# First two units of a mixture-of-experts layer routed inside the stage before it

## The reference, cut to what matters

```python
x = x + attn_a(layernorm(x))     # softmax attention + causal linear attention, one projection
x = x + ffn(layernorm(x))        # the feed-forward the change is about
x = x + attn_b(layernorm(x))     # state-space scan
x = x + ffn(layernorm(x))

def ffn(x):
    shared = (silu(x @ sw1) * (x @ sw2)) @ sw3
    probs = softmax(x @ rw + rb)                  # 8 experts
    w, idx = top_k(probs, 2); w = w / sum(w)
    # every expert: (silu(x @ ew1[e]) * (x @ ew2[e])) @ ew3[e], weighted by its gate
    return shared + routed
```

## Time and profile before

| what | value |
|---|---|
| median of three runs | 1902.08 us (1888.44 to 1910.78) |
| the profiled execution, its own time | 1923.11 us |
| its span | 1921.4 us |
| granted TensorE clock, mean | 0.843 |
| TensorE busy | 1397.9 us, 73% |
| VectorE busy | 1270.6 us, 66% |
| ScalarE busy | 847.5 us, 44% |
| GpSimd busy | 879.2 us, 46% |

### The profile page before, as it was taken

One profiled execution on the slowest core, in us unless ns is written; L12 is line 12 of the kernel. 1 busy time (PEld: TensorE's weight loads), 2 busy tenths in 40 slices (PEclk: granted clock), 3 DMA queues, 4 the chain that ended last, 5 costly groups with the idle time before them and its releaser, 6 DMA issues. The chain is left out here.

```text
span 1921.4 us, 27825 instructions
## 1 busy us (share of the span) xinstructions
PE 1397.9 (73%) x8207; PEld 699.9 (36%) x8208; DVE 1270.6 (66%) x2979; ACT 847.5 (44%) x1215; POOL 879.2 (46%) x773
## 2 busy tenths in 40 slices
PE   3459999999999996666884786675875454556883
PEld 1113333333332564445773221221321112435772
DVE  4667999998993566533332388999989995523333
ACT  3404666666667341112442677485573321112441
POOL 3401121121123553652554158879687664652552
PEclk9657999999999897787997797787886666877997
DMA  4721111111121325212223476958859635214225
GB/s 133 232 81 40 49 60 42 56 54 43 61 67 36 87 79 154 65 63 81 78 77 102 141 187 174 235 156 213 200 137 237 153 110 153 64 57 126 76 75 153
DMA packets 218312, 210.68 MB, mean 110 GB/s; under 512 B 49247, under 2 KB 188482, under 8 KB 215874
## 3 DMA queue, kind: packets, MB, share of 16 engines
q1 hardware_dynamic: 196174, 180.70, 35.0%
q0 software_dynamic: 9216, 19.02, 3.0%
q10 hardware_dynamic: 12800, 9.46, 1.6%
HBM read 145.27 MB, written 63.37 MB: 109 GB/s over the span
## 5 line engine op out<-in xcount | busy, mean ns | idle before, releaser
L804 ACT ACTIVATE attn_prob<-attn_ps_cols 128x1024 f32<-128x1024 f32 (+1 forms) x320 | 292.0, 940 | 219.6 <-PE attn_ps_cols L680 218.6
L2386 POOL TENSOR_TENSOR ssm_hc<-ssm_h,ssm_cb 128x1024 f32<-128x1024 f32 x128 | 300.8, 2357 | 137.3 <-DVE ssm_h L2369 113.5
L2369 DVE TENSOR_TENSOR_SCAN ssm_h<-ssm_decay,ssm_ps_u 128x1024 f32<-128x1024 f32 x128 | 292.7, 2287 | 30.9 <-ACT ssm_decay L2357 15.2
L830 POOL TENSOR_SCALAR_AFFINE_SELECT attn_prob<-attn_prob 128x512 f32<-128x512 f32 x128 | 81.2, 634 | 415.9 <-ACT attn_prob L804 415.9
L712 DVE CUSTOM_DVE_ANT_0 attn_ps_rows<-attn_ps_rows,const_mask_rows 128x384 f32<-128x384 f32 (+3 forms) x512 | 236.1, 523 | 39.5 <-PE attn_ps_rows L647 37.4
L647 PE MATMUL attn_ps_rows<-attn_ks,attn_qs 72*128 72x512 bf16 (+3 forms) x768 | 228.9, 352 | 44.2 <-DMA attn_qs<-parts_dram 30.9
L2357 ACT ACTIVATE ssm_decay<-ssm_wide,ssm_aneg 128x1024 f32<-128x1024 f32 x128 | 146.0, 1146 | 173.3 <-DVE ssm_h L2369 97.1
L2320 PE MATMUL ssm_ps_u<-ssm_stack,ssm_spread 96*128 96x512 bf16 x256 | 97.3, 471 | 154.3 <-DVE ssm_h L2369 148.1
L680 PE MATMUL attn_ps_cols<-attn_qs,attn_ks 75*128 75x512 bf16 (+3 forms) x768 | 194.4, 334 | 4.6 <-DMA attn_qs<-attn_nrows 3.9
L699 PE MATMUL attn_ps_o<-attn_prob,attn_vw 128*32 128x512 f32 (+3 forms) x1536 | 166.6, 507 | 0.3 <-POOL attn_prob L830 0.3
L717 DVE TENSOR_REDUCE attn_nm<-attn_ps_rows 128x1 f32<-128x512 f32 x256 | 157.8, 682 | 7.8 <-PE attn_ps_rows L647 7.7
(11 more groups left out here) (340 smaller groups left out, 2515.4 us busy)
## 6 DMA issues: line engine op xcount, KB each, us to landing
ssm_wide<-delta_dram SPq DMA_DIRECT2D x128, 512.0 KB, 6.3
attn_ks<-parts_dram SPq DMA_DIRECT2D x48, 192.0 KB
attn_qs<-parts_dram SPq DMA_DIRECT2D x48, 192.0 KB
parts_dram<-proj_parts SPq DMA_DIRECT2D x8, 768.0 KB, 3.8
ffn1e_x<-ex_dram SPq DMA_DIRECT2D x40, 130.0 KB
ffn2e_x<-ex_dram SPq DMA_DIRECT2D x40, 130.0 KB
split_dram<-ssm_parts SPq DMA_DIRECT2D x6, 768.0 KB, 4.4
ssm_stack<-split_dram SPq DMA_DIRECT2D x18, 256.0 KB, 4.6
```

Of the source, the lines that this page charges most:

```text
L804: nc.scalar.activation(prob[u % RING][:, heads[0]:heads[-1] + 1, 0:w], ps_cols[s % 2][:].rearrange("p b (x q) -> p (b x) q", x=len(heads) ...
L2369: nc.vector.tensor_tensor_scan(h[t % H_RING][:], decay[t % DECAY_RING][:], ps_u[t % 2][:], 0.0, ALU.mult, ALU.add).then_inc(scan_done, 1)
L2386: nc.gpsimd.tensor_tensor(hc[:, t % HC_RING, :], h[t % H_RING][:], cb[b % 2][:], ALU.mult).then_inc(hc_done, 1)
```

## The change

- The routing of the first feed-forward gets its own object, `Router`, which holds its tiles and semaphores and outlives a stage. For the first feed-forward it is made before the attention and holds the buffers of the first two units (`AHEAD_UNITS = 2`).
- The memory stage routes units 0 and 1. Their steps stand at fixed t in the lists of the engines, and use `ps_p` as PSUM tile for transpose, logits and counts; the transposes of the keys and the projections that write the same tile get waits. All sixteen scatters of the two units are issued there by GpSimd, at t = 24 to 31.
- The routing stage of the first feed-forward starts with unit 2 (`first = 2`): it loads units 2 to 7, scatters 48 times, and makes the shared products of all 8 units, those of unit 0 first. The inverse roots come in other groups (`AHEAD_ENDS`): units 0, 1, 2, 3 and 4, 5 and 6, 7; before they were 0, 1 and 2, 3 and 4, 5 to 7.
- `choose_dve` is cut in two, `choose_dve` and `settle_dve`, which stand one behind the other in the routing stage. The second feed-forward runs the new code from unit 0, in the order of before.

```diff
+TURNED_BEHIND = {5: 1, 7: 2}
@@ memory, turn_ka(half)
+            if half == 6:
+                nc.tensor.wait_ge(r.xT_ready, 2)
+            if half in TURNED_BEHIND:
+                nc.tensor.wait_ge(r.logits_ready, TURNED_BEHIND[half])
@@ memory, project_half(half)
+            if half == HALVES - 2:
+                nc.tensor.wait_ge(r.row_ready, AHEAD_UNITS)
+                nc.tensor.wait_ge(r.count_ready, AHEAD_UNITS)
@@ memory, SP, behind load_batch(2)
+                    if i == 2:
+                        load_choice(sp, r, a)
+                        for u in range(AHEAD_UNITS):
+                            sp.wait_ge(x1_stored[u], 16)
+                            sp.sem_inc(passed_sp, 1)
+                            sp.dma_start(r.x[u][:], dram["x1"][u * UNIT:(u + 1) * UNIT, :].rearrange("(j p) d -> p j d", p=P)).then_inc(r.x_loaded[u], 16)
@@ memory, TensorE, end of step t
+                    if t == 15:
+                        pe.wait_ge(x1_ready, 3)
+                        turn_pe(nc, r, c, 0)
+                    if t == 16:
+                        pe.wait_ge(r.r_loaded, 2 * 16)
+                        logits_pe(nc, r, 0)
+                    if t == 19:
+                        pe.wait_ge(r.set_up, 3)
+                        pe.wait_ge(x1_ready, 4)
+                        rank_pe(nc, r, 0)
+                    if t == 20:
+                        pe.wait_ge(r.row_ready, 1)
+                        pe.wait_ge(r.count_ready, 1)
+                        turn_pe(nc, r, c, 1)
+                    if t == 23:
+                        pe.wait_ge(x1_ready, 5)
+                        logits_pe(nc, r, 1)
+                    if t == 27:
+                        pe.wait_ge(x1_ready, 6)
+                        rank_pe(nc, r, 1)
@@ memory, VectorE, end of step t
+                    if t == 9:
+                        set_up_dve(nc, r, c, dve)
+                    if t in (12, 15):
+                        mean_dve(nc, r, dve, (t - 12) // 3)
+                    if t in (13, 16):
+                        norm_dve(nc, r, dve, (t - 13) // 3)
+                    if t == 17:
+                        dve.wait_ge(r.r_loaded, 2 * 16)
+                    if t in (17, 24):
+                        choose_dve(nc, r, dve, (t - 17) // 7)
+                    if t in (18, 25):
+                        settle_dve(nc, r, dve, (t - 18) // 7)
+                    if t in (19, 27):
+                        place_dve(nc, r, dve, (t - 19) // 8)
+                    if t in (20, 28):
+                        label_dve(nc, r, dve, (t - 20) // 8)
@@ memory, ScalarE, end of step t
+                    if t in (14, 17):
+                        twin_act(nc, r, act, (t - 14) // 3)
+                    if t in (15, 20):
+                        turned_act(nc, r, act, (t - 15) // 5)
+                    if t in (19, 26):
+                        tanh_act(nc, r, act, (t - 19) // 7)
@@ memory, GpSimd, end of step t
+                    if t == 2:
+                        set_up_pool(nc, r)
+                    if t in (12, 15):
+                        rstd_pool(nc, r, pool, (t - 12) // 3)
+                    if 24 <= t < 28:
+                        for j in range(2):
+                            scatter(nc, r, dram, pool, 0, (t - 24) * 2 + j)
+                    if 29 <= t:
+                        for j in {29: (0, 1), 30: (2, 3), 31: (4, 5, 6, 7)}[t]:
+                            scatter(nc, r, dram, pool, 1, j)
@@ route, TensorE
+                pe.wait_ge(s_loaded, 3 * 16)
+                for u in range(first - 1):
+                    share_pe(u, 0)
+                    share_pe(u, 1)
+                for s in range(first, UNITS_IN + 2):
...
@@ route, VectorE
+                for u in range(first, first + 3):
+                    mean_dve(nc, r, dve, u)
+                    if u == first:
+                        norm_dve(nc, r, dve, u)
+                for u in range(first - 1):
+                    share_dve(dve, u, 0)
+                    share_dve(dve, u, 1)
+                choose_dve(nc, r, dve, first)
+                settle_dve(nc, r, dve, first)
+                norm_dve(nc, r, dve, first + 1)
...
@@ route, GpSimd
+                for u in range(first, UNITS_IN):
+                    for j in range(TOP * UPT):
+                        scatter(nc, r, dram, pool, u, j)
+                    if group + 2 + u - first < len(r.ends):
+                        rstd_pool(nc, r, pool, group + 2 + u - first)
```

More of the change, by code:

```diff
@@ new lines, in label_dve, with turn_pe @@
+def label_dve(nc, r, dve, u):
+    k = u % DEEP
+    nc.vector.tensor_copy(r.xn[k][:, :, :, TOKEN].bitcast(I32), r.ids[:, :, u * UPT:(u + 1) * UPT]).then_inc(r.id_ready, 1)
+    dve.wait_ge(r.tanh_ready, u + 1)
+    nc.vector.tensor_scalar(r.xn[k][:, :, :, GATE], r.tanh[:], 0.5, 0.5, ALU.mult, ALU.add).then_inc(r.gate_ready, 1)
+def turn_pe(nc, r, c, u):
+    nc.tensor.wait_ge(r.xn_ready, u * UPT + UPT)
+    nc.tensor.wait_ge(r.xT_ready, u)
+    for j in range(UPT):
+        done = nc.tensor.transpose(r.ps_x[:, j * P:(j + 1) * P], r.xn[u % DEEP][:, 0, j, 0:D], c["ident"][:])
+    done.then_inc(r.xT_made, 1)
@@ new lines, in logits_pe, with rank_pe @@
+def logits_pe(nc, r, u):
+    nc.tensor.wait_ge(r.xT_ready, u + 1)
+    nc.tensor.wait_ge(r.logits_ready, u)
+    for j in range(UPT):
+        done = nc.tensor.matmul(r.ps_r[:, j, :], r.xnT[u % 2][:, j * P:(j + 1) * P], r.rw[:], start=True, stop=True)
+    done.then_inc(r.r_done, 1)
+def rank_pe(nc, r, u):
+    nc.tensor.wait_ge(r.chosen_ready, u + 1)
+    nc.tensor.wait_ge(r.count_ready, u)
+    nc.tensor.matmul(r.ps_k[:], r.before[:], r.chosen[:], start=True, stop=True)
+    for j in range(UPT):
+        done = nc.tensor.matmul(r.ps_k[:, j + 1:, :], r.ones[:], r.chosen[:, j:j + 1, :].broadcast_to([P, UPT - j, EXPERTS]),
+                                start=False, stop=True, skip_group_check=True)
+    done.then_inc(r.ranked, 1)
@@ L1295, in route, with set_up_dve @@
+def set_up_dve(nc, r, c, dve):
+    dve.wait_ge(r.ready, 5)
+    nc.vector.tensor_copy(r.before[:], c["strict"][:, 0, :]).then_inc(r.set_up, 1)
+    for free in (r.region, r.count):
+        nc.vector.tensor_scalar(free[:], r.number[:, 0, :], float(REGION), None, ALU.mult).then_inc(r.set_up, 1)
+def route(nc, dram, c, a, stage, src, w, w_loaded, t, r):
     with ExitStack() as ctx:
         m = Mem(nc, ctx, stage)
[L1297 to L1298 removed]
@@ L1306, in route @@
[L1306 to L1314, removed]
@@ L1315, in route @@
-        rowf, pos = m.sb("rowf", [P, TOP, UPT]), [m.sb(f"pos{k}", [P, TOP, UPT], I32) for k in range(DEEP)]
+        if r is None:
+            r = Router(m, dram[stage + "_sent"], GROUP_ENDS)
+            r.signals()
+        first = len(r.x)
+        r.grow(m, DEEP)
+        count = r.count
+        sw1, sw3 = m.sb("sw1", [P, 2, HIDDEN]), m.sb("sw3", [P, HC, D])
         act1 = [m.sb(f"act{h}", [P, UNIT]) for h in range(HC)]
@@ L1326, in route @@
-        x_loaded, stored = [m.sem(f"x_ld{k}") for k in range(DEEP)], m.pair("stored")
-        stat, mean, veps_ready, rstd_ready, xn_ready, xT_made = (m.sem(n) for n in ("stat", "mean", "veps", "rstd", "xn", "xT_made"))
-        xT_ready, r_done, logits_ready, top_ready, index_ready, order_ready = (m.sem(n) for n in ("xT", "r_done", "logits", "top", "index", "order"))
-        gap_ready, tanh_ready, gate_ready, pick_ready, chosen_ready = (m.sem(n) for n in ("gap", "tanh", "gate", "pick", "chosen"))
@@ L1585, in _ @@
+                    if s == first + 2:
+                        for u in range(first + 5, UNITS_IN):
+                            mean_dve(nc, r, dve, u)
                     if 1 <= s <= UNITS_IN:
@@ L1590, in _ @@
             def _(act):
-                for s in range(UNITS_IN + 1):
+                for u in range(first - 1):
+                    silu_act(act, u, 0)
+                    silu_act(act, u, 1)
+                for s in range(first, UNITS_IN + 1):
                     if s < UNITS_IN:
-                        turned_act(act, s)
+                        turned_act(nc, r, act, s)
                     if s >= 1:
```

424 lines of the change are left out of this document (213 added, 211 removed).

## The result

Over twenty runs of each the kernel before takes 1905.68 us and the kernel after 1896.86 us (medians); the ratio is 0.9949, 95% interval 0.9928 to 0.9969. The forecast was 1893 us and 0.9952. The total was right by luck: its two large terms were each off by some 8 us, one against the other.

A forecast was written before the change was run, and what follows sets the result against it. TensorE was taken to bound the memory stage, a chain with 64 scatters and dry spells the routing stage. Memory 10.8 us longer, routing 20 shorter: -9.2 us, 1893 us on the median of 1902.08; range 1875 to 1914.

The forecast's parts named there:

- TensorE's own work: Memory stage: a transpose, logits and rank for each of two units, all on the bound, 3.7 us longer.
- The roots: Memory stage, steps 12 and 15: GpSimd's inverse roots delay masks TensorE needs, by 2.5 and 1.8 us, together 4.3.
- The transpose at step 17: Memory stage: the transpose of keys waits for VectorE to make the first logits, 0.8 us (0 to 1).
- VectorE's steps: Memory stage: some 7 us a unit, overrun of 1 us in steps 18 and 19 hidden; uncovered, about 2 us.
- third rival: Shared port: VectorE's moved work and GpSimd's masks block each other, 4 us more, sum -5, 1897 us; chance 0.15.
- The scatters: Memory stage: 0.5 us from steps 24 to 27, later steps making it good, and 1.5 us at the end.
- The head: Routing stage start to first scatter of unit 2: that scatter at 768 instead of 788.75, 20.7 us earlier.
- From there to the last: Routing stage, first scatter of unit 2 to last: 78.1 us in the trace, 75 or 81 by dry spells' places.
- The end: Routing stage after the last scatter: counting, padding and barrier, the last 14.2 us, stay.
- rival 1: Routing stage without dry spells, GpSimd running through: 35 us earlier, sum -24, 1878 us; chance 0.15.
- The second, held signals in the memory stage: Engines held during scatters there: 22 to 25 us on top of 10.8, sum +14, 1916 us; chance 0.12.
- The fourth: Routing stage: TensorE's steps of 8 to 10 us set the end; gain about 14, sum -3, 1899 us; chance 0.13.

The follow-up runs named there:

- scatters_at_head: Kernel after with the sixteen scatters of units 0 and 1 moved from the memory stage to the routing stage's head; 1909.03 us, ratio 0.9968.
- base_unwaited: Kernel after with eight buffers for the shared sum and no VectorE wait for their stores, both feed-forwards; 1905.07 us, one run.
- the pause experiments: roots_later plus idle GpSimd fills behind every eighth, every fourth or each unit's fourth scatter, one with longer fills; 1863.19 to 1885.09 us.
- after_again: Kernel after, unchanged, run again, on chip 14; 1903.31 us, ratio 0.9940.
- roots_later: Kernel after with both inverse roots of the memory stage one step later on GpSimd (t = 13 and 16); 1893.09 us, ratio 0.9877.
- second_root_later: Kernel after with only the second inverse root of the memory stage one step later (t = 12 and 16); 1895.62 us, one run.
- pause_4: roots_later with an unused GpSimd fill of 1200 elements behind every fourth scatter in both routing stages; 1863.19 us, ratio 0.9759.
- before_pause_4: Kernel before with only the fills of pause_4 added in both routing stages, on chip 1; ratio 1.0159.
- pause_4_short: pause_4 with 200 elements in each fill, on chip 1; ratio 0.9948.

## Why the prediction was right, step by step

*Memory stage, +10.8 forecast, +18.6 measured.*
- TensorE's own work, 3.7: right (the transpose has 0.66, the logits of unit 1 1.06, the rank 0.24; the logits of unit 0 took 1.71 in the stretch of low clock).
- The roots, 4.3: **mis-sized**. The waits were 2.41 and 2.23 (forecast 2.5 and 1.8), but the step stopped there. They cost 9.0 in after by the rows, 8.2 and 9.1 by experiment, since the clock fell behind them. I had quoted 0.93 as the stage's clock and 0.50 for the next, and priced every added microsecond at full clock.
- The transpose at step 17 waiting for the logits, 0.8: it is 0.5.
- VectorE's steps, hidden: right. One wait of TensorE of 0.3 us for its masks, near step 20, where the cast of the row numbers took 1.22 us beside GpSimd's mask (its median elsewhere is 0.17). That is the third rival's mechanism, as the Trainium skill, SBUF — State Buffer, "SBUF: two separate sides", describes it; the trace agrees at that one cast, and it cost 0.3, not 4.
- The scatters, 0.5 + 1.5: **mis-sized**, 5.1 by scatters_at_head. The end was 2.3 us longer (751.26 to 762.49, before 735.59 to 744.48), near the 2.6 that I had as its upper bound. The steps at the end didn't make good what steps 24 to 27 lost: from the mask of block 28 to that of 31 it is 11.2 us, before 9.4, with a pair of scatters in two of the three steps.

*Routing stage, -20 forecast, -28.7 measured (-25.5 to -28.7 over the kernels with this stage).*
- The head, 23.5 us to the first scatter of unit 2: 22.5.
- From there to the last, 78.1: **mis-sized**, 71.7, in the other kernels up to 74.9. The dry spells kept their places but were shorter. The new groups put a root behind unit 3, and VectorE's held instruction went on at 809.59, 1.8 us behind the end of that root (1.9 in base_unwaited); the pause experiments show that an operation between scatters of this length can let the signals through. The first dry spell is 3.9 to 4.6 us, not 8.6, in every kernel with this stage. The second is 6.1 and 6.6 us in after and after_again alone, and 8.6 to 8.7 in roots_later, second_root_later and base_unwaited, with the same operations: what shortened it isn't shown, and some 3 of the 6.4 us hang on it. The prediction had the pair of observations (the first sixteen scatters, with a root between, held nobody) and used it for rival 1 alone.
- The end, unchanged at 15.2 us from the last scatter's start: 13.7.

*The rivals.* The first (no dry spells, stage 35 us shorter) didn't come by this change, but pause_4 shows on chip 0 what a stage without them takes: 99.7 us with eleven fills. The second, held signals in the memory stage, came small: one remote wait, 2.5 us late, and a part of the 1.8 us in steps 28 to 31. The memory stage came within 1.4 us of the 20 from which this rival was to decide, though mostly by the roots. The argument against it, that the products of the experts' loops go on beside the scatters, overlooked that ScalarE's copies there wait late. The fourth is out on the chips with late signals: what TensorE's steps take was never the end of a unit once signals passed.

Shown by experiment: the price of the roots' place, the price of the scatters in the memory stage, that the remote waits for the shared sum aren't waits for stores, and that fills behind every fourth scatter remove nearly all of them. Argued only: how the 9.0 us in after divide between wait and clock, and that the root behind unit 3 shortened the first dry spell, some 4 of the 8 us that this stage gained beyond the forecast. Open: what holds the signals, why on chips 0 and 14 and not on chip 1, how short a pause may be, and what the change gives on chip 1.

The fastest kernel on chip 0 is pause_4, 0.9759 of before. On chip 1 its fills of 1 us would by estimate cost what they cost in before_pause_4, 0.98 each; pause_4_short won 0.5% there and wasn't run on chip 0.

## What to carry to other kernels

When an engine that is the bound gets a wait, price the wait and then what its clock does behind it: here 4.6 us of waits became 8 to 9. A wait can often be moved for nothing by putting the waiting instruction one step later on its own queue. And when two engines resume at the same moment, a fixed time after a run of indirect DMAs, try a pause in that run before moving work out of it: on chip 0 eleven and fifteen idle fills gave more (0.9877 to 0.9759) than routing two units ahead had given (0.9949), on chip 1 they only cost. So compare kernels on one chip, and note which.

## What was not expected of the hardware

- In a run of sixteen scatters from GpSimd without another operation between, VectorE and ScalarE waited 14.8 and 16.7 us for TensorE, VectorE's product being finished for 14.1 of them, and went on together, 2.65 us after the last scatter. With 1.1 us of another GpSimd operation behind every fourth, the longest wait for the shared sum was 2.8 us.
- It isn't on every chip. On chips 0 and 14 it shows; on chip 1 the kernel before takes 1803.64 us instead of some 1912, no wait in the routing and experts' stages of the profiled kernels is remote, and the fills only cost their time.
- The same memory stage took 141.13 us in one execution and 144.25 us in two, and began at 0.69 and 0.80 of the clock in the first (20 us), at 0.55 and 0.59 in the others. The version of roots_later took 132.95 and 135.18 us with the same two beginnings.
